# Copying a table from DRAM to DRAM instead of through SBUF, with the dst order read earlier and products of zeros in an idle stretch of TensorE

## The chip, the core and the metric

One core of one Trainium2 chip runs the kernel. The metric is the device time of one execution in microseconds (us), lower is better. The engines are TensorE (PE in the profile, PEld its weight loads), VectorE (DVE), ScalarE (ACT), GpSimd (POOL) and SyncE (SP), which only issues DMA transfers; 16 DMA engines move the data. A name with q behind it (SPq) is the engine's queue of DMA issues.

## The reference

A graph network of two layers over N = 50000 nodes with 256 features and 12500 edges; `src` and `dst` are the edges' ends, and `dst` comes sorted.

```python
h = x @ Wn.T + bn;  e = edge_attr @ We.T + be                 # layer 0, edge_attr is 12500 x 128
a = leaky_relu(sum((h[src] + e) * attn, -1), 0.01)
a = softmax of a over the edges with the same dst
z = x + relu(segment_sum(h[src] * a, dst))
x1 = layernorm(z)
mean = segment_mean(x1[dst], over the edges with the same src)  # layer 1
r = x1 + x1 @ W1.T + b1 + mean @ W2.T + b2
out = layernorm(r)
```

## The kernel before

Edges lie in T = 100 tiles of 128, four tiles make a quad, Q = 25. Nodes lie in G = 98 groups of 512, a group being 128 partitions of four rows (4 KB). All engines run in parallel, each in its own written order, held together by semaphores. The stages are:

1. *Edge features.* SyncE loads `edge_attr` in 12 blocks of eight tiles and two single ones; VectorE makes a dot product of each tile with a vector (`features`, L754), into `pay`. Before, VectorE and ScalarE make one-hots of the dst keys (`onehots`, `high_onehots`), and TensorE counts them (`sort`, first half).
2. *Sort by dst, then by src* (`sort`, `tiles`). For each quad SyncE loads the low digits of its keys (`low_digits_scratch` into `lowB`, which is part of `aggn`) and the keys (`keys_scratch` into `kB`), spread over all partitions. TensorE looks up and counts (L1228, L1179), VectorE makes ranks. GpSimd scatters each tile's (dst, src, dot) to its rank in `order_scratch` (L473), `FLIGHT` in flight, and reads the order back. The one-hots of src are made between the two.
3. *Gathers of x rows* by the dst order (`X<-in_x`, L464), `FLIGHT` in flight. They start when the dst order has been read and turned, which VectorE does in the src tiles at quad `ORDER_AT` and the two after; a row of `X` is free once the src tile in it has been counted. VectorE then makes a dot product of each tile with `v_b`, and the softmax follows.
4. *Adds* (`by_dst`). TensorE sums each quad's rows by dst and multiplies by Wn, ScalarE cuts at zero, GpSimd adds the result to rows of `z_scratch` by indirect DMA (L513), a quad after the adds of the quad before have landed.
5. *All nodes* (`dense`). Each group is loaded from `z_scratch`, normalised, turned, multiplied by W1 and I, normalised and stored. Meanwhile the src order is scattered and read (`HOOK`), and rows of z are gathered for the neighbours (`s_nb`).
6. *The rows that have edges by src* (`by_src`) once more, with the mean of the neighbours, scattered over `out`.

`z_scratch` must hold x before the first add. SyncE copies it there, a group at a time, with a load into `yout` and a store two steps later, each waiting for an earlier one (`copy`). The copy is cut up and its parts stand between SyncE's other issues: 4 steps at the start, `COPY_FIRST` ahead of the fifth block of edge features, one after the keys of two quads in three, `COPY_ONEHOTS` after the keys of the first src quad, the rest after the first two loads of the sorted dst keys. SyncE issues in this order, and what stands behind a wait waits too. GpSimd waits for the last stores ahead of its first add.

Of the kernel before, what the change touches and what calls it, by code (L numbers as in the profile page):

```python
# [20 lines left out]
BF16 = mybir.dt.bfloat16  # L21
I32 = mybir.dt.int32
DST, SRC = 0, 1
ORDER_AT = 12
FLIGHT = 4
COPY_FIRST = 12
COPY_ONEHOTS = 14
HOOK = 24


def wait(eng, sem, value):

    if isinstance(value, int) and value <= 0:
        return
    eng.wait_ge(sem, value)
# [19 lines left out]
def build(nc, x, src, dst, edge_attr, Wn, bn, We, be, attn, W1, b1, W2, b2, out):  # L55
# [12 lines left out]
    assert 2 * HC <= 512 and LO == 2 * P and T % 4 == 0  # L68
    EC = 2 * GT
    NEC = FT // EC  # L70

    z_dram = nc.dram_tensor("z_scratch", [N + 6 * P, D], F32).ap()
    keyrow_dram = [nc.dram_tensor(f"keys_scratch{k}", [T, P], F32).ap() for k in (DST, SRC)]
# [4 lines left out]
    with ExitStack() as ctx:  # L78
# [6 lines left out]
        def sems(name, n):  # L85
            return [sem(f"{name}{i}") for i in range(n)]
# [142 lines left out]
        s_sortd = sem("sorted_keys_in_dram")  # L229
        s_xones = sem("ones_columns")  # L230
        s_xg = sems("src_rows_gathered", FLIGHT)
        s_cin = sems("copy_loaded", 4)
        s_cout = sems("copy_stored", 4)
        s_zero = sem("spare_rows_cleared")

        s_xin = sems("x_loaded", 4)
# [43 lines left out]
        s_enm = sem("edge_r_scales")  # L280
        s_ey = sem("edge_y_ready")
        s_xs = sems("own_z_rows_gathered", 4)
        s_nb = sems("neighbour_z_rows_gathered", 2)
        s_zsc = sems("z_rows_added", 4)
        s_ysc = sems("y_scattered", 4)
        s_rc = sems("reciprocals", 6)
# [10 lines left out]
        def grp(dram, g, parts=P):  # L297

            if isinstance(g, int):
                return dram[g * GN:g * GN + parts * GT].rearrange("(p j) d -> p (j d)", j=GT)  # L300
            return dram[0:(G - 1) * GN].rearrange("(g p j) d -> p g (j d)", p=P, j=GT)[:, bass.ds(g, 1), :] \
                .rearrange("p a f -> p (a f)")
# [13 lines left out]
        def parts(g):  # L316
            return LP if isinstance(g, int) and g == G - 1 else P
# [4 lines left out]
        def full(ap):  # L322
            return ap[:].rearrange("p j d -> p (j d)")
# [4 lines left out]
        @block.sync  # L328
        def _(sp):
            sp.wait_ge(s_const, 1)  # L330
            for k, key in ((DST, dst), (SRC, src)):
                sp.dma_start(keyrow_i[k][0:FT, :], key[0:FT * P].rearrange("(t p) -> t p", p=P)).then_inc(s_krow[k], 16)
            for w, t in ((Wn, 0), (W1, 1), (W2, 2)):
                sp.dma_start(xin[t][:, 0:2, :], w.rearrange("(b p) k -> p b k", b=2)).then_inc(s_w, 16)
            sp.dma_start(weT, We.rearrange("(b p) k -> p b k", b=2)).then_inc(s_w, 16)

            copied = [0]

            def copy(n):

                for c in range(copied[0], min(copied[0] + n, G + 2)):
                    if c < G:
                        wait(sp, s_cout[c % 4], 16 * (c // 4))
                        sp.dma_start(full(yout[c % 4])[0:parts(c)], grp(x, c, parts(c))).then_inc(s_cin[c % 4], 16)
                    if c >= 2:
                        h = c - 2
                        sp.wait_ge(s_cin[h % 4], 16 * (h // 4 + 1))
                        sp.dma_start(grp(z_dram, h, parts(h)), full(yout[h % 4])[0:parts(h)]).then_inc(s_cout[h % 4], 16)
                copied[0] = min(copied[0] + n, G + 2)

            copy(4)
            sp.wait_ge(s_wt, 3)
            sp.wait_ge(s_vu, 1)

            for c in range(NEC):
                if c == 4:
                    copy(COPY_FIRST)
                wait(sp, s_eau, EC * (c - 3))
                v = edge_attr[0:NEC * EC * P].rearrange("(c t p) d -> p c t d", p=P, t=EC)
                sp.dma_start(full(xin[c % 4]).rearrange("p (t d) -> p t d", d=DE),  # L360
                             v[:, c:c + 1].rearrange("p a t d -> p (a t) d")).then_inc(s_ea[c % 4], 16)
            c = NEC
            for t in range(NEC * EC, FT + 1):
                rows = P if t < FT else LT
                sp.wait_ge(s_eau, EC * (c - 3))
                sp.dma_start(xin[c % 4][0:rows, 0, 0:DE], edge_attr[t * P:t * P + rows]).then_inc(s_ea[c % 4], 16)
                c += 1


            for k in (DST, SRC):  # L370
                sp.wait_ge(s_keyd[k], 32)
                for q in range(Q):
                    n = k * Q + q
                    wait(sp, s_lbT, n - 1)
                    wait(sp, s_lbA, n - 1)
                    sp.dma_start(lowB[n % 2], spread(lowrow_dram[k], q)).then_inc(s_lb[n % 2], 16)
                    wait(sp, s_kbu, n - 1)
                    sp.dma_start(full(kB[n % 2]), spread(keyrow_dram[k], q)).then_inc(s_kb[n % 2], 16)
                    if k == SRC and q == 0:
                        copy(COPY_ONEHOTS)  # L380
                    elif q % 3:
                        copy(1)

            def load3(k, q):
                if k == DST and q < 2:
                    sp.wait_ge(s_kbu, 2 * Q)
                if k == SRC and q < 2:
                    sp.wait_ge(s_sel[DST], Q)
                wait(sp, s_sel[k], q - 1)
                sp.dma_start(full(kB[q % 2]), spread(sorted_dram[k], q)).then_inc(s_kb3[k][q % 2], 16)  # L390

            sp.wait_ge(s_sortd, 16)
            for q in range(2):
                load3(DST, q)
            copy(G + 2)
            for q in range(2, Q):
                load3(DST, q)

            for u in range(4):
                sp.wait_ge(s_zsc[u], 16 * GT * len(range(u, Q, 4)))  # L400

            def dense(g, m, u):
                if in_range(g, 0, G):
                    n = parts(g)
                    if in_range(g, 4, G):
                        wait_apart(sp, s_tp, 2 * (g - 4) + 2)
                    sp.dma_start(full(xin[u])[0:n], grp(z_dram, g, n)).then_inc(s_xin[u], 16)
                if in_range(g, 5, G + 5):
                    h, hu = g - 5, (u - 5) % 4
                    n = parts(h)  # L410
                    wait_apart(sp, s_y, GT * h + GT)
                    sp.dma_start(grp(out, h, n), full(yout[hu])[0:n]).then_inc(s_yst[hu], 16)
                if isinstance(g, int) and g == G - 6:
                    sp.wait_ge(s_sortd, 32)
                    for q in range(2):
                        load3(SRC, q)
            steps(sp, G + 5, 4, 5, 12, dense)

            for q in range(2, Q):
                load3(SRC, q)  # L420
# [3 lines left out]
        def _(pool):  # L424
# [35 lines left out]
            def column(idx, t):  # L460
                return bass.IndirectOffsetOnAxis(ap=idx[:, t:t + 1], axis=0)

            def gather(dst_ap, table, where, s):
                g.indirect_dma_start(out=dst_ap, out_offset=None, in_=table, in_offset=where).then_inc(s, 16)  # L464
# [31 lines left out]
            def order_src(n):  # L496

                pool.wait_ge(s_rank, 2 * Q)
                for t in range(sent[0], min(sent[0] + n, T)):
                    scatter_order(SRC, t)  # L500
                sent[0] = min(sent[0] + n, T)

            order_src(20)
            for u in range(4):
                pool.wait_ge(s_cout[u], 16 * len(range(u, G, 4)))
            pool.wait_ge(s_zero, 48)

            for q in range(Q):
                pool.wait_ge(s_relu, 2 * q + 2)
                if q:  # L510
                    pool.wait_ge(s_zsc[(q - 1) % 4], 16 * GT * ((q - 1) // 4 + 1))
                for j in range(GT):
                    g.indirect_dma_start(out=z_dram, out_offset=column(idx_out[DST], GT * q + j), in_=xin[q % 4][:, j, :],  # L513
                                         in_offset=None, compute_op=ALU.add).then_inc(s_zsc[q % 4], 16)
                order_src(2)

            for h in range((T - sent[0]) // 2):
                pool.wait_ge(s_x1, GT * h + GT)
# [4 lines left out]
            pool.wait_ge(s_agg[DST], T)  # L523
            for t in range(T):
                pool.wait_ge(s_x1, GT * (HOOK + 8 + (G - HOOK - 14) * t // T))
                wait(pool, s_nb[t % 2], 16 * (t // 2))
                gather(X[:, t, 0:D], z_dram, column(idx_dst[SRC], t), s_nb[t % 2])

            for q in range(Q + 3):
                if q < Q:  # L530
# [209 lines left out]
        def _(dve):  # L740
# [295 lines left out]
                ins.then_inc(s_nst, 1)  # L1036

            def first_neighbours():
                for par in range(2):
                    dve.wait_ge(s_nb[par], 16 * len(range(par, T, 2)))  # L1040
                for q in range(2):
                    neighbour_stats(q, q)

# [104 lines left out]
        def _(pe):  # L1148
# [47 lines left out]
            def sort(k, after):  # L1196
# [3 lines left out]
                for t in range(T):  # L1200
# [2 lines left out]
                        pe.wait_ge(s_hotA, k * Q + t // GT + 1)  # L1203
                    count_tile(hist, t)
                nothing(hist, start=False, stop=True).then_inc(s_hist, 1)

                pe.wait_ge(s_rowtot, k + 1)
                tot = scanned[:, :, HC - 1:HC].rearrange("p b c -> p (b c)")
# [189 lines left out]
```

## Time and profile before

| | us |
|---|---|
| time before, median of 3 runs | 1667.97 (1666.65 to 1668.83) |
| the profiled execution | 1660.1 |
| its span in the profile | 1658.3 |
| TensorE busy | 1265.2 (76%) |
| VectorE busy | 1094.4 (66%) |
| ScalarE busy | 782.0 (47%) |
| GpSimd busy | 750.0 (45%) |
| granted TensorE clock, mean share of the full one | 0.901 |

The shares are means over stages with different limits, so the rows below go by stage. In a view of windows each line is a stretch in us from the span's start, with each engine's busy time and its count of instructions, the granted TensorE clock (1.00 is 2.4 GHz, 0.50 is 1.2 GHz), the mean busy share of the 16 DMA engines and what they moved. In the chain of waits a line is a start, a duration and what lasted; a DMA's duration there runs from its issue to its landing. A releaser is the event that ended an engine's idle time.

### The profile page before, as it was taken

To read this page: it belongs to the slowest core of one execution; us is meant where nothing else is said; L and a number is where in the kernel's file an instruction comes from. 1 tells how busy PE (TensorE), PEld (TensorE's weight loads), DVE (VectorE), ACT (ScalarE), POOL (GpSimd) and SP (SyncE) were. 2 spreads that over 40 slices of the span, in tenths; PEclk is the share of its full clock that TensorE was granted. 3 is DMA by queue.
4 is the path that set the end of the run, shared out by engine and by line. 5 is a ranking of instruction groups with operands and counts; after the bars stand their busy time and mean duration, and the time that the engine had idled before them with its cause. 6 is when DMAs were issued, how large, how long until landed. Compare 5 with 4: busy or idle time off the path is not lost.

```text
span 1658.3 us, 26818 instructions
## 1 busy us (share of the span) xinstructions
PE 1265.2 (76%) x7210; PEld 1068.7 (64%) x7210; DVE 1094.4 (66%) x3970; ACT 782.0 (47%) x1768; POOL 750.0 (45%) x731
## 2 busy tenths in 40 slices
PE   4277865776000799985099999999999899999994
PEld 3166754665000688764088888888888688877784
DVE  8565585666322655441088888888888888777762
ACT  6243475442000344332067777777777455444442
POOL 1035652035555678788642013333332256555553
PEclk9688798998555899999599999999999999999997
DMA  8977588767999555554557678888887323232221
GB/s 286 300 185 214 172 261 268 234 228 236 335 343 344 141 83 83 82 70 51 95 179 223 218 237 265 263 269 267 262 271 254 128 80 98 87 95 88 90 81 46
DMA packets 134006, 311.40 MB, mean 188 GB/s; under 512 B 24605, under 2 KB 57972, under 8 KB 133928
## 3 DMA queue, kind: packets, MB, share of 16 engines
q1 hardware_dynamic: 91870, 245.02, 44.7%
q0 software_dynamic: 40128, 64.45, 18.2%
q10 hardware_dynamic: 1930, 1.06, 0.2%
q8 instruction: 28, 0.46, 0.1%
q14 instruction: 50, 0.41, 0.1%
HBM read 182.23 MB, written 129.96 MB: 188 GB/s over the span
## 4 chain that ended last, share of the span: by engine, by line
PE 44%; DMA 27%; POOL 12%; issue 8%; DVE 4%; ACT 2%; SPq 2%; POOLq 0%; ACTq 0%
PE bank L1250 25%; DMA aggn<-low_digits_scratch 7%; DMA X<-in_x,idx_src 7%; PE bank L1240 6%; DMA z_scratch<-yout 5%; POOL z_scratch L513 4%; DMA xin<-z_scratch,idx_src 4%; POOL out_rows L467 4%; POOL xin L464 3%; PE bank L1247 3%; PE bank L1228 3%; DMA z_scratch<-xin,idx_out 3%; PE bank L1295 2%; PE bank L1291 2%; PE bank L1179 1%
## 5 line engine op out<-in xcount | busy, mean ns | idle before, releaser
L1250 PE MATMUL bank<-w1T,xT 128*128 128x256 f32 x1968 | 490.7, 380 | 0.0
L1250 PEld LDWEIGHTS bank<-w1T,xT 128*128 128x128 f32 x1968 | 343.3, 190 | 66.3
L473 POOL DMA_INDIRECT order_scratch<-pay,rank_i x200 | 196.8, 984 | 230.6 <-DVE rank_i L846 95.9
L568 ACT ACTIVATE yout<-bank,nmr,rstd 128x256 f32<-128x256 f32 x492 | 251.2, 576 | 8.0 <-DVE nmr L754 8.0
L919 DVE BATCH_NORM_STATS2 stats<-xin 128x6 f32<-128x512 f32 x246 | 158.7, 686 | 111.3 <-DMA xin<-z_scratch 57.6
L559 ACT COPY xT<-bank 128x512 f32<-128x512 f32 x346 | 203.0, 588 | 36.3 <-PE bank L1240 25.0
L464 POOL DMA_INDIRECT X<-z_scratch,idx_dst x100 | 94.9, 949 | 257.1 <-DVE xin L751 191.1
L919 DVE BATCH_NORM_STATS2 stats<-bank 128x6 f32<-128x512 f32 x246 | 168.5, 694 | 59.9 <-PE bank L1250 59.5
L667 ACT COPY agg<-bank 128x257 f32<-128x257 f32 (+1 forms) x200 | 74.2, 371 | 219.3 <-PE bank L1295 212.5
L513 POOL DMA_INDIRECT z_scratch<-xin,idx_out x100 | 158.2, 1582 | 40.7 <-issue 26.9
L1179 PE MATMUL bank<-X 128*128 128x196 bf16 x800 | 100.1, 261 | 99.0 <-ACT sel L654 72.8
L1228 PE MATMUL bank<-sel,agg 128*128 128x196 f32 x800 | 175.4, 369 | 0.0
L1240 PE MATMUL bank<-ident,xin 128*128 128x128 f32 x984 | 132.2, 274 | 53.1 <-DVE xin L751 53.1
L751 DVE TENSOR_SCALAR xin<-xin,stats,rstd 128x256 f32<-128x256 f32 x492 | 171.5, 410 | 1.0
L464 POOL DMA_INDIRECT X<-in_x,idx_src x100 | 97.1, 971 | 160.3 <-DVE idx_out L905 76.6
L563 ACT ACTIVATE std<-stats,eps_c 128x4 f32<-128x4 f32 x271 | 81.0, 300 | 182.0 <-DVE stats L919 173.8
L1247 PE MATMUL bank<-bias,ones 128*128 128x256 bf16 (+1 forms) x592 | 161.5, 273 | 3.0 <-ACT xT L559 2.7
L467 POOL DMA_INDIRECT out_rows<-yout,idx_out x100 | 99.9, 999 | 140.4 <-DMA xin<-z_scratch,idx_src 68.1
L1240 PEld LDWEIGHTS bank<-ident,xin 128*128 128x128 f32 x984 | 117.3, 142 | 68.3 <-issue 53.5
L1228 PEld LDWEIGHTS bank<-sel,agg 128*128 128x128 f32 x800 | 152.6, 218 | 0.3
L1179 PEld LDWEIGHTS bank<-X 128*128 128x128 bf16 x800 | 69.1, 102 | 128.2 <-ACT sel L654 86.5
L1295 PE MATMUL bank<-agg,csel 128*128 128x257 f32 (+1 forms) x396 | 123.4, 393 | 29.5 <-ACT agg L667 29.3
(187 smaller groups left out, 1911.7 us busy)
## 6 DMA issues: line engine op xcount, KB each, us to landing
yout<-in_x SPq DMA_DIRECT2D x97, 512.0 KB, 6.1
z_scratch<-yout SPq DMA_DIRECT2D x97, 512.0 KB, 7.1
xin<-z_scratch SPq DMA_DIRECT2D x97, 512.0 KB, 5.2
out_rows<-yout SPq DMA_DIRECT2D x97, 512.0 KB, 3.4
kB<-keys_scratch SPq DMA_DIRECT2D x50, 256.0 KB, 5.1
kB<-sorted_scratch SPq DMA_DIRECT2D x50, 256.0 KB, 3.4
aggn<-low_digits_scratch SPq DMA_DIRECT2D x50, 128.0 KB, 7.1
xin<-in_edge_attr SPq DMA_DIRECT2D x12, 512.0 KB, 7.1
```

Source lines behind the costliest of these rows:

```text
L464: g.indirect_dma_start(out=dst_ap, out_offset=None, in_=table, in_offset=where).then_inc(s, 16)
L473: g.indirect_dma_start(out=order_dram[k], out_offset=bass.IndirectOffsetOnAxis(ap=rank_i[k][:, t:t + 1], axis=0), in_=pay[:, t, :], in_off ...
L513: g.indirect_dma_start(out=z_dram, out_offset=column(idx_out[DST], GT * q + j), in_=xin[q % 4][:, j, :], in_offset=None, compute_op=ALU.ad ...
L559: a.copy(xT[dst_i][:].rearrange("p a b c -> p (a b c)"), src_bank[:, :]).then_inc(copied, 1)
L568: a.activation(yout[hu][0:rows, j, :], bank_of(j // 2)[0:rows, (j % 2) * D:(j % 2 + 1) * D], ACT.Identity, bias=nmr[0:rows, slot, j:j + 1] ...
L751: return v.tensor_scalar(o, i, s1, s2, o0, o1) if o1 is not None else v.tensor_scalar(o, i, s1, s2, o0)
L919: return v.bn_stats(stats[0:rows, slot, 2 * p:2 * p + 2, :].rearrange("p j s -> p (j s)"), pair.rearrange("p j c -> p c j"))
L1179: ins = mm(o[:, b * HC:(b + 1) * HC], onehot_lo[:, t, b * P:(b + 1) * P], onehot_hi[:, t, :], start=False, stop=False, skip_group_check=True)
L1228: ins = mm(bank[3 + t % 4][:, 0:HC], onehotT[n % 2][:, b, j * P:(j + 1) * P], table[i % 2][:, b, :], start=b == 0, stop=b == 1)
L1240: ins = tr(o[:, at:at + n], buf[0:n, 2 * p + jj, c * P:(c + 1) * P], ident[0:n, 0:n])
L1247: mm(to, ones16[:, 0:n], bias16[:, bias, :], start=True, stop=False)
L1250: ins = mm(to, buf[:, jj, c, 0:n], w[:, c, :], start=False, stop=i == len(terms) - 1 and c == 1)
```

## The change

The copy goes from DRAM to DRAM in NCOPY = 100 transfers, each of 125 rows of 4 KB that lie 400 nodes apart. SyncE waits for none of them; GpSimd waits for all before its first add. Eight stand ahead of the fifth block of edge features, one after each dst quad's keys, 24 after the keys of the second src quad (two at a time, as VectorE's one-hots of src progress), one after every second src quad's keys from the fourth on, and the 32 left after the first two loads of sorted dst keys. The four steps at the start are gone. `ORDER_AT` goes from 12 to 5, `FLIGHT` from 4 to 6, `HOOK` from 24 to 48; the neighbour gathers have four semaphores instead of two; GpSimd's order scatters leave the loop of the adds. After the counting of the dst keys TensorE makes 72 products of zeros into a bank that nothing reads, six after the first dot of each block.

```diff
-ORDER_AT = 12
-FLIGHT = 4
-COPY_FIRST = 12
-COPY_ONEHOTS = 14
-HOOK = 24
+ORDER_AT = 5
+FLIGHT = 6
+HOOK = 48
...
+    NCOPY = 100
...
-            copy(4)
             sp.wait_ge(s_wt, 3)
             sp.wait_ge(s_vu, 1)
+            def part_of(table):
+                return table.rearrange("(r c k) d -> c r (k d)", c=NCOPY, k=GT)
+            def copy_x(n):
+                for c in range(copied[0], min(copied[0] + n, NCOPY)):
+                    sp.dma_start(part_of(z_dram[0:N])[c], part_of(x)[c]).then_inc(s_copy, 16)
+                copied[0] = min(copied[0] + n, NCOPY)
             for c in range(NEC):
                 if c == 4:
-                    copy(COPY_FIRST)
+                    copy_x(8)
...
-                    if k == SRC and q == 0:
-                        copy(COPY_ONEHOTS)
-                    elif q % 3:
-                        copy(1)
+                    if k == DST or q >= 2 and q % 2:
+                        copy_x(1)
+                    if k == SRC and q == 1:
+                        for i in range(Q // 2):
+                            sp.wait_ge(s_onehot, Q + 2 * i + 1)
+                            copy_x(2)
...
-            copy(G + 2)
+            copy_x(NCOPY)
...
             order_src(20)
-            for u in range(4):
-                pool.wait_ge(s_cout[u], 16 * len(range(u, G, 4)))
+            pool.wait_ge(s_copy, 16 * NCOPY)
...
-                order_src(2)
...
-                wait(pool, s_nb[t % 2], 16 * (t // 2))
-                gather(X[:, t, 0:D], z_dram, column(idx_dst[SRC], t), s_nb[t % 2])
+                wait(pool, s_nb[t % 4], 16 * (t // 4))
+                gather(X[:, t, 0:D], z_dram, column(idx_dst[SRC], t), s_nb[t % 4])
...
                 nothing(hist, start=False, stop=True).then_inc(s_hist, 1)
+                if k == DST:
+                    for c in range(NEC):
+                        pe.wait_ge(s_eau, EC * c + 1)
+                        for _ in range(6):
+                            nothing(bank[0][:, 0:2 * HC], start=True, stop=True)
```

## Rows read from the trace of the kernel before

**Rows 1.** Windows view by stage; PE, PEld, DVE, ACT, POOL busy, clock, DMA share, GB/s.
```profile
22.00:87.00 65.00, 20.94 (x197) 15.91 (x194) 44.51 (x306) 33.14 (x93) 0.00 (x0) 0.77 0.96 302
87.00:225.00 138.00, 104.89 (x587) 95.33 (x588) 83.16 (x439) 56.06 (x98) 76.15 (x77) 0.82 0.67 190
225.00:282.00 57.00, 32.75 (x255) 25.59 (x254) 38.12 (x189) 39.20 (x107) 23.72 (x24) 0.89 0.95 297
282.00:409.00 127.00, 95.08 (x582) 86.10 (x580) 82.97 (x442) 53.50 (x93) 36.10 (x37) 0.92 0.72 231
409.00:564.00 155.00, 17.77 (x78) 13.24 (x79) 59.28 (x278) 6.10 (x15) 80.42 (x84) 0.55 0.91 311
564.00:822.00 258.00, 195.49 (x1032) 160.86 (x1030) 95.48 (x353) 87.33 (x188) 207.00 (x150) 0.92 0.55 72
822.00:1286.00 464.00, 456.47 (x2676) 385.28 (x2677) 408.65 (x1066) 331.46 (x758) 129.46 (x137) 0.99 0.75 247
```

**Rows 2.** SyncE's first issues; GB/s in 40 slices from 3.5 to 5.5 us.
```profile
1.13 0.35 SPq L332 DMA_DIRECT2D keyrow_i<-in_dst  x1
...
2.12 2.73 SPq L334 DMA_DIRECT2D xin<-in_L_gnn_Wn  x1
...
GB/s 5 21 25 24 24 23 32 22 22 22 22 22 21 21 32 21 21 22 23 23 24 24 33 42 42 21 21 38 41 20 31 20 20 20 20 21 20 20 20 41
```

**Rows 3.** DMA from 29 to 33 us, windows view from 28, DMA from 62 to 84.
```profile
DMA packets 447, 1.62 MB, mean 405 GB/s; under 512 B 51, under 2 KB 53, under 8 KB 446
...
28.00:44.00 16.00, 9.34 (x91) 6.95 (x88) 15.78 (x75) 16.00 (x47) 0.00 (x0) 1.00 0.96 342
...
DMA packets 9175, 6.04 MB, mean 274 GB/s; under 512 B 223, under 2 KB 8755, under 8 KB 9174
```

**Rows 4.** Timeline, chain and windows view around the edge features.
```profile
24.12 1.73 SPq L344 DMA_DIRECT2D yout<-in_x  x1
...
45.66 0.08 DVE L754 DVE_READ_ACCUMULATOR xin<-xin,u_b 128x1 f32 x1
...
54.51 0.33 PE L1175 MATMUL bank<-zero 128*128 128x392 bf16 x1
...
61.85 7.65 DMA xin<-in_edge_attr
...
80.38 3.91 DVE xin L754 x36
...
84.00:88.00 4.00, 1.69 (x5) 1.43 (x6) 2.86 (x13) 1.44 (x2) 0.00 (x0) 0.50 0.73 257
...
87.32 1.67 PE L1212 MATMUL bank<-csel,ident 128*128 128x392 f32 x2 [1.04 <-DVE csel L754]
```

**Rows 5.** Chain of waits in the dst tiles, two of its low digit loads.
```profile
155.40 7.44 DMA aggn<-low_digits_scratch
...
172.54 7.41 DMA aggn<-low_digits_scratch
```

**Rows 6.** Timeline at the start of the src tiles, ScalarE and SyncE.
```profile
282.29 0.72 ACT L606 ACTIVATE aggn<-aggn,slot_f 128x512 bf16<-128x512 bf16 x1 [3.07 <-DMA aggn<-low_digits_scratch]
...
284.06 0.32 SPq L378 DMA_DIRECT2D kB<-keys_scratch  x1
...
292.49 0.32 SPq L378 DMA_DIRECT2D kB<-keys_scratch  x1
```

**Rows 7.** The gathers of x rows, by tile X from 340 to 540 us.
```profile
L464 POOL DMA_INDIRECT X<-in_x,idx_src x100: 940/946/1196, 348.0 to 527.8; - x100
...
DMA to landing us min/median/max: 2.7/6.3/9.5
```

**Rows 8.** Timeline of GpSimd at the first add and around a quad's.
```profile
563.95 1.63 POOL L513 DMA_INDIRECT z_scratch<-xin,idx_out  x1 [4.90 <-ACT xin L680]
...
695.01 1.57 POOL L513 DMA_INDIRECT z_scratch<-xin,idx_out  x1 [0.30 <-issue]
...
699.60 1.61 POOL L513 DMA_INDIRECT z_scratch<-xin,idx_out  x1 [0.43 <-ACT xin L680]
```

More of the change, by code:

```diff
@@ L70, in build @@
     NEC = FT // EC
+    NCOPY = 100
+    assert N % (NCOPY * GT) == 0
     z_dram = nc.dram_tensor("z_scratch", [N + 6 * P, D], F32).ap()
@@ L231, in build @@
         s_xg = sems("src_rows_gathered", FLIGHT)
-        s_cin = sems("copy_loaded", 4)
-        s_cout = sems("copy_stored", 4)
+        s_copy = sem("x_copied")
         s_zero = sem("spare_rows_cleared")
@@ L282, in build @@
         s_xs = sems("own_z_rows_gathered", 4)
-        s_nb = sems("neighbour_z_rows_gathered", 2)
+        s_nb = sems("neighbour_z_rows_gathered", 4)
         s_zsc = sems("z_rows_added", 4)
@@ L335, in _ @@
             sp.dma_start(weT, We.rearrange("(b p) k -> p b k", b=2)).then_inc(s_w, 16)
[L337 to L349, printed above, removed]
-            copy(4)
             sp.wait_ge(s_wt, 3)
             sp.wait_ge(s_vu, 1)
+            copied = [0]
+            def part_of(table):
[4 more added lines that the diff above has]
+                copied[0] = min(copied[0] + n, NCOPY)
             for c in range(NEC):
                 if c == 4:
-                    copy(COPY_FIRST)
+                    copy_x(8)
                 wait(sp, s_eau, EC * (c - 3))
@@ L1038, in first_neighbours @@
             def first_neighbours():
-                for par in range(2):
-                    dve.wait_ge(s_nb[par], 16 * len(range(par, T, 2)))
+                for i in range(4):
+                    dve.wait_ge(s_nb[i], 16 * len(range(i, T, 4)))
                 for q in range(2):
```

## The prediction

> **What bounds the kernel now.** First the page: span 1658.3 us, of which TensorE 76%, no engine near full, so the stages are read apart. The windows view [rows 1] shows two kinds. From 822 to 1286 us TensorE is busy 457 of 464 us, and what comes after is touched by no edit. Ahead of it, from 22 to 564 us, no engine is full, but the DMA engines are at 0.96, 0.67, 0.95, 0.72 and 0.91. From 564 to 822 us GpSimd is busy 207 of 258 us, the most of all.
>
> The chain and the issues say what the front half waits for. From 24.1 to 61.85 us SyncE is held in the copy, whose loads and stores wait for each other; the fifth block of edge features is issued only then, lands at 69.5 us, and the dots end at 84.3 us [rows 4]. In the dst tiles one low digit load in three comes late, behind two copy pairs: its 7.4 us are on the chain once in each 17.1 us, that is three quads [rows 5]. Between the tiles of dst and of src 14 copy steps hold SyncE, and the low digits of the third src quad land at 282.3 us [rows 6]. Where no load is late two quads take 8.43 us, 4.2 each [rows 6]; over the stage it is 5.5. The x row gathers run from 348 to 534 us, four in flight at 6.3 us each [rows 7], under 311 GB/s in all [rows 1]. From 564 us a quad of adds takes 10.3 us: GpSimd 7.4 for four, then the landing of the last, under which lie two order scatters [rows 8].
>
> **The change, part by part.** *The copy.* 98 loads and 98 stores go; 100 transfers from DRAM to DRAM of 125 rows of 4 KB come. Bytes through the DMA engines fall from 102.4 to 51.2 MB, and SyncE waits for no piece. The question is how many of the 16 DMA engines a piece runs on. The rows say this depends on the count of rows: two loads of 97 rows, the first issued at 1.13 us, fill 3.5 to 5.5 us at 20 to 25 GB/s in most slices, and SyncE needs 2.73 us to issue the next load; transfers of 128 rows move 405 GB/s in 29 to 33 us, 16 times 25.3, and 274 GB/s where nearly all packets are of 512 bytes, as those of the 97 rows are [rows 2, 3]. So 97 rows ran on one engine, 128 on all. 97 is prime; the simplest reading of both is that rows are dealt out in equal shares. 125 rows then go to five engines of 25 rows. I forecast that.
>
> The Trainium skill, DMA: Bandwidth & Descriptors, on why a DMA increments its semaphore by 16, has the same as a rule: the number of engines is the largest one up to 16 that divides the slowest dimension of both sides, always the lowest-numbered. By it too this change is to be feared, and the trace's 97 rows agree.
>
> A packet of 4 KB costs an engine 162 ns at 405 GB/s and 191 ns at 342 [rows 3]; 25 of them 4.05 to 4.8 us. No row shows DRAM to DRAM. The two rates are 18% apart by nothing but how well the transfers follow each other, and pieces that wait for nothing may follow better still: I allow half of that again below, 3.7. Above, a read and a write one after the other would make 8.1 to 9.6. I take one pass and 4.4 us, the middle. Everything SyncE issues stands behind it on those five engines: key and low digit loads of a quad (384 KB) take them 1.0 us, order scatters about 0.5 (an estimate: the DMA share is 0.67 at 190 GB/s with them and 0.72 at 231 almost without, 0.08 of 138 us more than the bytes explain, over 25 quads [rows 1]).
>
> Now the sum, by stages.
> 1. *Edge features.* Eight pieces, 35 us from 24.3, behind blocks already issued: 61. The fifth block, issued at 45.7 once the first block's dots are done [rows 4], lands at 64.5 instead of 69.5: **-5 us** (-7 to -2).
> 2. *Zero products.* TensorE makes 72 of 392 columns while idle (from 54.8 us); at 0.33 us for one [rows 4] they are 24 us, spread over the dots, six after each block's first, so the last six end about with the dots. The clock is 0.50 from 84 to 88 us [rows 4]; the seed takes 1.67 us there, and half at the full clock. **-1 us** (-2 to 0; a TensorE still busy at the end would cost 1).
> 3. *Dst tiles*, one piece in each quad. Five engines: 4.4 + 1.0 + 0.5 = 5.9 us, above the 4.2 of the work, so 25 quads take 148 us against 138: **+10**. The stage ends at 229, not 225.
> 4. *Src one-hots.* SyncE issues 24 pieces ahead of the low digits of the third quad. 24 x 4.4 = 106 us, with landing and rest 109.5: these arrive at 338.5, not 282.3. ScalarE's one-hots (35 us from 226) and two quads fill only the first 45 us. **+52**.
> 5. *Src tiles* with 11 pieces. Five engines in two quads: 4.4 + 2.0, and from the eighth quad 2.5 for seven gathers; 9 us, 4.6 a quad with slips, 23 quads 107 us against 127: **-20**. They end at 446.
> 6. *To the first add.* The dst order read at quad 5 not 12 lets gathers start in the eighth quad, at 366, and six in flight let GpSimd set the pace, 0.95 us each and 0.3 between [rows 7, 8]: done by about 495, logits and softmax by 525 (30 us from the last landing to the first add, as before [rows 7, 8]). But GpSimd's adds wait for all 100 pieces, and key loads of the third and later quads are queued behind them: 32 x 4.4 = 141, gathers 12, scatters and keys 4, 1.5 to start: 604.5, where it was 563.95. 158.5 us against 155: **+3.5**. The early gathers are worth nothing here, they are 80 us ahead of the copy.
> 7. *Adds.* Without the order scatters the landing sets the pace: the last add is issued at 695.01 and lands 3.8 later by the chain, and the next quad starts at 699.60, only 0.43 after the second scatter's end [rows 8]. At most 0.3 us a quad: **-2** (-8 to 0). The 50 scatters go to the next stage, where GpSimd is busy 129 of 464 us [rows 1]; 80 of them, two a group, end at group 40, and the load of the order has eight groups of 4.7 us (464 us for 98) to HOOK 48.
> 8. *Neighbour gathers.* 100 in 36 groups rather than 60: one in 1.7 us, and GpSimd's 0.95 [rows 7] fits. DMA load there rises from about 0.8 to 0.9; TensorE covers it: 0 (to +5 if x loads come late).
>
> Sum -5 -1 +10 +52 -20 +3.5 -2 = **+37.5 us**. The profiled execution took 1660.1 us (span 1658.3), 7.9 under the median of 1667.97; I add the difference to the median: **1705.5 us**. At 4.05 us a piece the same steps give +1.5, at 4.8 us +74, so this case reaches 1669 to 1742. It breaks even near 4.03 us, 161 ns a packet: close to the best measured rate.
>
> **Rivals.** *All 16 engines.* If 125 rows are spread like 128, a piece takes 1.3 to 1.5 us. Then dots end 16 us sooner, 25 dst quads take 109 us, 24 pieces (36 us) hide under ScalarE's one-hots, src tiles end near 329 and gathers, from 254 at 1.26 us, near 385; the first add comes 30 us later at 415: -149 -2, **1517 us**. With two passes (3.0 us a piece) the copy ends at 475: **1578**. For it: no row shows a count like 125, and the one narrow case ran among the small loads of the start; against it, its flat 21 GB/s at a packet size that elsewhere gives 274. 0.22.
> *Faster on five engines.* A piece under 4.0 us: a queue of plain copies with nothing waiting between could run at the 405 GB/s slices' better half. 3.7 us gives -34, **1635**. 0.10; the 0.04 about break-even make no change.
> *Two passes on five engines.* Read and write share the engine's time: 8.1 us and more, 97 us later for each us: +397, **2065 us**. No row excludes it: in every row one side is on chip. 0.18. The Trainium skill, DMA: Bandwidth & Descriptors, latency and other measured facts, gives 214 GB/s each way for copies between HBM tensors on all engines; by that a piece on five would take 7.7 us. No run here shows it yet.
> *One engine for 125 rows*, 22 us a piece, past 3000 us: 0.01. *The move of the order matters, the copy not*: needs a copy that ends by 525, so 3.5 us a piece or all 16 engines; contained above.
>
> **How the numbers follow.** Forecast (five engines, one pass, slower) 0.42, two passes 0.18, one engine 0.01 and 0.03 for a price between one pass and two make slower 0.64; faster is 0.22 + 0.10 = 0.32; same 0.04. Within 0.2%, 3.3 us, is what a measurement here can't tell from no change. Predicted is the likeliest, 1706 us, its own range 1669 to 1742. The range of eight in ten takes in the 16-engine rival and the five-engine cases up to 5.3 us a piece: 1515 to 1790; two passes are left out.
>
> **What would show it.** In the profile after: DMA share near 5/16 = 0.31 with about 110 GB/s while only pieces run (30 to 45 us); the low digits of the third src quad landing near 338 us; GpSimd idle for over 50 us before its first add, released by the copy, near 604; gathers done near 495. A share near 1 while pieces run and a first add near 415 prove the 16-engine rival; about 65 GB/s at such a share and a first add near 960, two passes. A packet 10 ns off moves the result by 24 us, so the sign hangs on that price.

## Result and profile after

| | us |
|---|---|
| after, median of 4 runs | 1708.11 (1703.05 to 1712.09) |
| before beside it, 4 runs | 1667.64 (1666.65 to 1668.83) |
| ratio, 95% interval | 1.0241 (1.0213 to 1.0269) |
| profiled execution, span | 1703.05, 1701.3 |

Slower by 40 us, as forecast (1706, +37.5). Executions of one kernel fall into a fast and a slower state; a ratio with an interval, here and below, is of fast ones alone, a median without one is of all runs.

The windows of the kernel after, with the columns of [rows 1]:

```profile
22.00:80.00 58.00, 37.31 (x277) 23.87 (x274) 44.44 (x306) 34.54 (x97) 0.00 (x0) 0.94 0.66 195
80.00:227.00 147.00, 102.54 (x603) 91.64 (x603) 87.71 (x457) 59.27 (x107) 90.95 (x94) 0.91 0.57 155
227.00:331.00 104.00, 30.45 (x244) 23.28 (x244) 34.57 (x173) 36.36 (x100) 7.41 (x8) 0.70 0.34 125
331.00:473.00 142.00, 103.39 (x572) 95.34 (x573) 82.62 (x438) 53.12 (x93) 79.06 (x83) 0.82 0.62 176
473.00:611.00 138.00, 17.04 (x71) 11.96 (x69) 49.25 (x259) 5.57 (x13) 39.36 (x38) 0.56 0.38 145
611.00:870.00 259.00, 198.19 (x1040) 163.72 (x1040) 97.82 (x376) 88.38 (x189) 156.46 (x100) 0.92 0.54 72
870.00:1332.00 462.00, 453.58 (x2654) 382.58 (x2655) 405.80 (x1057) 329.51 (x752) 174.39 (x184) 0.99 0.74 246
```

Against [rows 1] the third stage is 104 us instead of 57, and the DMA share there is 0.34, not 0.95: the engines aren't full, yet everybody waits for a transfer. The DMA view of 30 to 45 us and of 520 to 600 us, where hardly anything but pieces runs, says how few engines work (the row of digits is the busy share of 40 slices in tenths):

```profile
DMA  3323233332323323333234332323333232332323
...
DMA packets 498, 1.97 MB, mean 132 GB/s; under 512 B 20, under 2 KB 20, under 8 KB 496
...
q1 hardware_dynamic: 496, 1.95, 32.0%
...
DMA packets 2959, 10.76 MB, mean 135 GB/s; under 512 B 264, under 2 KB 264, under 8 KB 2959
```

32.0% is 5.1 of 16 engines. Five engines at 132 GB/s are 26.4 GB/s each, or 155 ns for a packet of 4 KB. 25 packets are 3.88 us a piece, where I took 176 ns and 4.4 us. SyncE, the chain of waits and GpSimd show what stands behind the pieces:

```profile
23.90 19.27 SPq L346 DMA_DIRECT2D z_scratch<-in_x  x8
...
227.19 85.72 SPq L346 DMA_DIRECT2D z_scratch<-in_x  x24
...
472.69 120.92 SPq L346 DMA_DIRECT2D z_scratch<-in_x  x32
```
```profile
313.01 17.66 DMA aggn<-low_digits_scratch
...
390.99 10.12 DMA aggn<-low_digits_scratch
404.06 10.18 DMA aggn<-low_digits_scratch
417.03 10.82 DMA aggn<-low_digits_scratch
```
```profile
611.01 1.63 POOL L508 DMA_INDIRECT z_scratch<-xin,idx_out  x1 [87.36 <-DMA z_scratch<-in_x]
...
634.70 1.56 POOL L508 DMA_INDIRECT z_scratch<-xin,idx_out  x1 [3.04 <-DMA z_scratch<-xin,idx_out]
```

The issue of 24 pieces lasts from 227.19 to 312.91. The waits for one-hots between them can't be what holds SyncE: with the same waits the kernel with 128 rows issues its 24 pieces in 27.16 us (below). Its queue takes a new piece only as old ones move. The third src quad's low digits are issued behind it and land at 313.01 + 17.66 = 330.7, where they landed at 282.3 [rows 6]. The DMA views of 227 to 257 us and of 257 to 313 us show that these pieces began more slowly than they went on:

```profile
DMA packets 1047, 2.98 MB, mean 99 GB/s; under 512 B 316, under 2 KB 330, under 8 KB 1045
...
DMA packets 1869, 7.38 MB, mean 132 GB/s; under 512 B 70, under 2 KB 70, under 8 KB 1868
```

At 132 GB/s the first 30 us would have moved 3.96 MB, so some 7 us were lost there; why is not known. Ahead of its first add GpSimd stands 87 us for the copy. Added up from the front in the two profiled executions, in us later than before:

| place | before | after | later | forecast |
|---|---|---|---|---|
| edge feature dots end | 84.3 | 77.5 | -6.8 | -5 |
| dst tiles end | 225 | 227.2 | +2 | +4 |
| third src quad's low digits | 282.3 | 330.7 | +48.4 | +56 |
| first dot of a gathered tile, src tiles done | 408.9 | 473.9 | +65.0 | +36 |
| first add | 563.95 | 611.01 | +47.1 | +39.5 |
| first load of all nodes | 822.1 | 871.5 | +49.4 | +37.5 |
| end of the span | 1658.3 | 1701.3 | +43.0 | +37.5 |

### The profile page after: what moved, and what is told of

It is laid out like the page before. It is cut to its first block, busy times and chain, and to the rows that moved or that the text cites. A ratio compares the mean times of both kernels' runs of the same rounds, so it can differ in the third digit from the quotient of the medians.

```text
span 1701.3 us, 26861 instructions
## 1 busy us (share of the span) xinstructions
PE 1287.3 (76%) x7282; PEld 1083.0 (64%) x7282; DVE 1088.1 (64%) x3970; ACT 783.1 (46%) x1768; POOL 747.7 (44%) x731
## 4 chain that ended last, share of the span: by engine, by line
PE 36%; DMA 23%; POOL 12%; SPq 12%; DVE 8%; issue 7%; ACT 2%; POOLq 0%; ACTq 0%; DVEq 0%
PE bank L1249 23%; DMA aggn<-low_digits_scratch 12%; SPq L346 11%; PE bank L1239 6%; POOL z_scratch L508 6%; DMA z_scratch<-xin,idx_out 5%; POOL out_rows L463 4%; DMA xin<-z_scratch,idx_src 3%; DVE X L745 3%; POOL xin L460 3%; PE bank L1246 3%; PE bank L1294 1%; PE bank L1227 1%; DMA xin<-in_edge_attr 1%; PE bank L1290 1%
## 5 line engine op out<-in xcount | busy, mean ns | idle before, releaser
L913 DVE BATCH_NORM_STATS2 stats<-xin 128x6 f32<-128x512 f32 x246 | 158.5, 686 | 94.0 <-DMA xin<-z_scratch 56.6
L1290 PE MATMUL bank<-X,sel 128*128 (+2 forms) x400 | 123.7, 393 | 80.1 <-DVE csel L745 80.1
L1227 PE MATMUL bank<-sel,agg 128*128 128x196 f32 x800 | 179.4, 375 | 0.0
L1227 PEld LDWEIGHTS bank<-sel,agg 128*128 128x128 f32 x800 | 156.1, 222 | 0.3
```

Source lines behind the costliest of these rows:

```text
L913: return v.bn_stats(stats[0:rows, slot, 2 * p:2 * p + 2, :].rearrange("p j s -> p (j s)"), pair.rearrange("p j c -> p c j"))
L1227: ins = mm(bank[3 + t % 4][:, 0:HC], onehotT[n % 2][:, b, j * P:(j + 1) * P], table[i % 2][:, b, :], start=b == 0, stop=b == 1)
```

## Experiments

Three groups of four kernels, each group on one chip with before beside it. The first ran where before took 1656.68 us (1649.49 to 1664.59, 7 runs). In the second and third, on two other chips, before took 1729.12 (1677.02 to 1744.02) and 1720.37 us (1687.30 to 1753.12). In all eight profiles taken there the chain of waits from 60 to 600 us has 8 to 23% in "another core or an unknown queue", in the six of the first two chips nothing. So those kernels are compared with each other alone, without interval.

### First group: rows of a piece, place of the order, zeros

**128 rows.** The piece's rows, and nothing else: 97 pieces of 128 rows and one of 84.

```diff
-    NCOPY = 100
+    NCOPY = G
...
-                return table.rearrange("(r c k) d -> c r (k d)", c=NCOPY, k=GT)
+                if c == G - 1:
+                    return grp(table, c, LP)
+                return table[0:(G - 1) * GN].rearrange("(r c k) d -> c r (k d)", c=G - 1, k=GT)[c]
```

> The changed kernel, but with pieces of 128 rows (97 of them, and one of 84) at the same places. Theory (rows are dealt out in equal shares, so 125 rows ran on five engines and 128 run on 16; a packet costs 155 ns as in the changed kernel): a piece takes 1.3 to 1.5 us, the DMA share is near 1 and the rate near 400 GB/s from 25 to 33 us, the low digits of the third src quad land near 230 us, the first add comes near 415 us when the gathers and the softmax are done, and the time is 1520 to 1560 us. Rival (a copy from DRAM to DRAM is slow for another reason, such as reads and writes of the same memory, at 132 GB/s whatever the rows): the rate stays at 132 GB/s and the time near 1708 us. Rival two passes at 16 engines (3 us a piece): the first add near 475 us and 1578 us.

**1520.85 us** (1517.93 to 1523.14), ratio 0.9175 (0.9138 to 0.9213). Its DMA view from 30 to 38 us, its first add, and its windows for three of the stages:

```profile
DMA packets 786, 2.88 MB, mean 359 GB/s; under 512 B 88, under 2 KB 88, under 8 KB 784
...
q1 hardware_dynamic: 784, 2.85, 101.8%
```
```profile
428.31 1.63 POOL L509 DMA_INDIRECT z_scratch<-xin,idx_out  x1 [9.82 <-ACT xin L675]
```
```profile
180.00:234.00 54.00, 33.46 (x273) 26.18 (x271) 39.36 (x197) 39.60 (x108) 22.93 (x24) 0.95 0.96 257
234.00:341.00 107.00, 88.87 (x573) 80.18 (x573) 81.59 (x439) 53.43 (x93) 60.15 (x62) 0.94 0.71 211
341.00:422.00 81.00, 11.23 (x46) 7.73 (x46) 53.44 (x267) 3.73 (x9) 58.79 (x59) 0.56 0.75 269
```

All 16 engines are busy, the 24 pieces are issued in 27.16 us instead of 85.72, and the copy is gone from GpSimd's wait: the first add waits 9.8 us for the last step of its own chain. The number of engines that a piece runs on, not the copy from DRAM to DRAM as such, is what the change lost by.

**100 rows.** The changed kernel with `NCOPY = 125`, so pieces of 100 rows: more and smaller pieces, of a count that shares out over ten engines.

> The changed kernel with 125 pieces of 100 rows: the same numbers of pieces at the same places, 57 instead of 32 at the end. Theory (the largest number of engines up to 16 that divides the rows, so 10): 10 packets of 155 ns, 1.55 us a piece of 410 KB, 264 GB/s and a DMA share of 0.63 while only pieces run; first add near 437 us, about 1545 us. Rival (rows are cut into 16 shares rounded up, 15 engines of 7 rows, and 125 rows ran on five for another reason): 1.1 us a piece, 377 GB/s, share 0.94. Rival (five engines whenever the rows are no multiple of 16): 3.1 us a piece, 132 GB/s, share 0.32, and 1700 us or more.

**1541.21 us** (1539.51 to 1546.06), ratio 0.9303 (0.9262 to 0.9344). Its DMA view from 30 to 40 us, and its first add:

```profile
DMA packets 703, 2.63 MB, mean 263 GB/s; under 512 B 63, under 2 KB 63, under 8 KB 702
...
q1 hardware_dynamic: 702, 2.62, 64.3%
```
```profile
442.99 1.63 POOL L508 DMA_INDIRECT z_scratch<-xin,idx_out  x1 [30.18 <-DMA z_scratch<-in_x]
```

64.3% is 10.3 engines at 26 GB/s. So 125, 100 and 128 rows run on 5, 10 and 16 engines: equal shares, as the prediction read from 97 rows. The Trainium skill (DMA: Bandwidth & Descriptors, on why a DMA increments its semaphore by 16) states this as a rule, and these three runs agree with it. At ten engines GpSimd still waits for the copy, 30 us, and the kernel takes 20 us longer than on 16.

**Order at quad 12.** The changed kernel with `ORDER_AT = 12`.

> The changed kernel with ORDER_AT 12 as before. Theory (the copy on five engines ends last, everything about the gathers is ahead of it): the gathers of x rows start near 415 us instead of 364 and end near 545, the first add still comes at 611 us within 4, and the time is the same within 0.2%, 1705 to 1711 us. Rival (the early gathers crowd the five engines in the src tiles and slow the low digits there): the src tiles end 10 to 20 us sooner, and if the pieces after them aren't slower by the same, the time falls by as much.

**1709.41 us** (1707.21 to 1713.12), ratio 1.0308 (1.0263 to 1.0353). The windows and the first add:

```profile
326.00:461.00 135.00, 95.69 (x563) 87.17 (x564) 80.75 (x432) 53.51 (x93) 44.35 (x47) 0.86 0.52 150
461.00:611.00 150.00, 18.82 (x81) 13.61 (x78) 53.70 (x264) 5.56 (x13) 72.12 (x74) 0.56 0.46 164
```
```profile
611.66 1.63 POOL L508 DMA_INDIRECT z_scratch<-xin,idx_out  x1 [56.29 <-DMA z_scratch<-in_x]
```

Gathers begin at 398.0 instead of 363.7, and the first add comes at the time that the changed kernel had on the first chip. The late order moves time: the src tiles are 135 us instead of 142 with fewer gathers in them, and the stretch to the first add is 12 us longer. That the early order is worth nothing on five engines is not shown by this, since no run of the changed kernel stands beside it on that chip: by the ratios to before (1.0308 and 1.0241, the intervals just overlap) quad 12 is 11 us slower. The kernel without zeros, next, has its order at quad 5 and ran on the same chip. It issues the low digits of the third src quad at the same time (309.04 against 308.87), and has its first add at 602.85, 9 us before the one with quad 12 (one profiled execution of each, and its own was the fastest of its four); the medians are 6 us apart, with runs that just overlap. So the early order may be worth some 6 to 11 us even here. A likely reason is that with quad 12 more of the gathers share the engines with the last 32 pieces: 52 of them are issued between the first dot and the first add, and 18 in the changed kernel.

**No products of zeros.** The changed kernel without them:

```diff
-                if k == DST:
-                    for c in range(NEC):
-                        pe.wait_ge(s_eau, EC * c + 1)
-                        for _ in range(6):
-                            nothing(bank[0][:, 0:2 * HC], start=True, stop=True)
```

> The changed kernel without the products of zeros. Theory (they only warm the seed: 1.10 us against 1.67 us): the time is the same within 0.1%, at most 1 us longer. Rival (they keep TensorE's clock up into the dst tiles, where low digit loads are late): the dst tiles take several us longer without them, 1711 us or more.

**1703.49 us** (1698.26 to 1708.27), ratio 1.0282 (1.0235 to 1.0329). The one product behind the dots, in this kernel and in the changed one:

```profile
79.70 1.68 PE L1206 MATMUL bank<-csel,ident 128*128 128x392 f32 x2 [1.03 <-DVE csel L748]
```
```profile
80.09 1.10 PE L1211 MATMUL bank<-csel,ident 128*128 128x392 f32 x2 [1.03 <-DVE csel L748]
```

The zeros save 0.58 us there. The rival, a clock held up through the dst tiles, can be judged by the kernel with quad 12, which has the zeros and ran on the same chip. With and then without zeros the 24 pieces behind the dst tiles begin at the same time:

```profile
225.40 83.36 SPq L346 DMA_DIRECT2D z_scratch<-in_x  x24
...
224.83 84.10 SPq L346 DMA_DIRECT2D z_scratch<-in_x  x24
```

So the dst tiles are no longer without them, and that rival fell. For the total the interval overlaps the changed kernel's 1.0241, and a difference of a few us can't be told: no run of the changed kernel on that chip stands beside it.

### Second group: what limits it once the copy is quick

**The changed kernel again.**

> The changed kernel once more, beside the kernels with 128-row pieces and on the chip that runs them. If the zero products do nothing but heat TensorE's idle time, it is within 0.3% of the kernel without them, whose ratio was 1.028; if they hold the clock up behind the edge features, it is 4 us and more below that one. From the first measurement the ratio should be 1.024, some 40 us above before. The fixed part of each stage (dst tiles 147 us, src tiles 142 us, first add near 611) should come again within 2 us, since five DMA engines set them.

**1819.15 us** (1796.35 to 1824.08) where before took 1729.12: 1.052, and stages came later by tens of us, so the expectation of the same stages failed; the one on the zeros can't be judged across chips. A piece was no dearer (DMA from 30 to 40 us: 131 GB/s at 31.8%), but the first add came at 656.69.

**128 rows, order at quad 12** (`ORDER_AT = 12`).

> Pieces of 128 rows on all 16 engines, but the dst order read at quad 12 of the src tiles as in the kernel before. Theory: on five engines the early order was worth nothing because the copy ended 80 us behind the gathers; with the copy done by 240 us the gathers end last before the adds, so seven quads of 4.3 us later costs 25 to 30 us, less some 4 us because the src tiles are crowded by fewer gathers: 1543 to 1550 us against 1521 (ratio near 0.934), first add near 455. Rival: the order is worth nothing here either, since the gathers are bounded by the rows of X that the src tiles free: 1521 to 1525 us, first add near 430.

**1705.42 us** (1698.43 to 1727.52), first add at 542.79, where 1543 to 1550 and 455 were expected. The kernel with quad 5 and HOOK 48 did not run on this chip; the next one has quad 5, but HOOK 24.

**128 rows, order scatters back in the adds, HOOK 24:**

```diff
-HOOK = 48
+HOOK = 24
...
                                          in_offset=None, compute_op=ALU.add).then_inc(s_zsc[q % 4], 16)
+                order_src(2)
```

> Pieces of 128 rows, but the two order scatters of src stand between the quads of the adds again and the order of src is turned at group 24. Theory: the scatters lie under the landing of the adds, whose gap of 2.9 to 3.2 us in the version without them hardly shortens, so 25 quads give back 3 to 8 us: 1524 to 1529 us; the dense stage stays at 462 us, since TensorE sets its pace. Rival: the scatters cost nothing at all (1521), or the later order also eased DMA in the dense stage and its return makes this 10 us and more (1531 or over).

**1672.64 us** (1657.21 to 1682.70), first add at 524.21. The total has no partner here, so the pace of the adds has to decide. GpSimd's first add of two quads in this kernel, and in the one without the scatters:

```profile
741.93 1.61 POOL L509 DMA_INDIRECT z_scratch<-xin,idx_out  x1 [0.47 <-ACT xin L676]
...
752.11 1.61 POOL L509 DMA_INDIRECT z_scratch<-xin,idx_out  x1 [0.41 <-issue]
```
```profile
645.77 1.56 POOL L509 DMA_INDIRECT z_scratch<-xin,idx_out  x1 [3.06 <-ACT xin L675]
...
655.98 1.56 POOL L509 DMA_INDIRECT z_scratch<-xin,idx_out  x1 [3.05 <-DMA z_scratch<-xin,idx_out]
```

These are 10.18 and 10.21 us a quad, and over all 25 quads the mean is 10.35 with the scatters and 10.34 without: the scatters fill a gap of 3 us that the landing leaves anyway. In the adds the rival "nothing at all" holds, mine of 3 to 8 us fell.

**128 rows, order at quad 1, 16 pieces among the one-hots:**

```diff
-ORDER_AT = 5
+ORDER_AT = 1
...
-                        for i in range(Q // 2):
+                        for i in range(8):
                             sp.wait_ge(s_onehot, Q + 2 * i + 1)
                             copy_x(2)
```

> Pieces of 128 rows, the dst order read at quad 1 of the src tiles instead of 5, and 16 pieces instead of 24 among the one-hots of src (the other eight come after the sorted dst keys). Theory: the gathers set the first add, so four quads of 4.3 us earlier give 17 us, and eight pieces fewer ahead of the third quad's low digits up to 8 us more: 1496 to 1504 us, first add near 408. Rival: a row of X is free only when the src tile in it has been counted, so the gathers are held to the tiles' pace of 1.07 us each and more tiles of crowding slow the tiles: no more than 5 us won, 1515 to 1521, or slower.

**1662.41 us** (1651.77 to 1662.60), first add at 491.42: 43 us below the one with quad 12 and 10 below the one with quad 5 and HOOK 24. It differs from both by more than the order.

### Third group: four of them repeated

> The changed kernel, repeated beside its relatives, since on the last chip before itself spread from 1677 to 1744 us and loads there landed late. On a quiet chip: ratio 1.024 as first measured, first add near 611. If the ratio is 1.05 again, the changed kernel suffers more than the one before from whatever made that chip slow.

> Pieces of 128 rows, repeated as the base for the two below. Expected 0.9175 of before, 1521 us on a quiet chip, first add near 428.

> Pieces of 128 rows and the order read at quad 12. Theory: the gathers end last before the adds, so it is 25 to 30 us above the version with quad 5 (1546 to 1551), first add near 455. Rival: no difference, within 4 us of it.

> Pieces of 128 rows, the order read at quad 1, 16 pieces instead of 24 among the one-hots of src. Theory: 17 us from the gathers and up to 8 from the one-hots, 1496 to 1504 on a quiet chip, first add near 408. Rival: gathers held to the pace of the tiles, no more than 5 us won.

| kernel | us | gathers from, to | first add |
|---|---|---|---|
| changed | 1827.26 (1780.85 to 1843.89) | | 658.4 |
| 128 rows, order at 5 | 1672.89 (1670.69 to 1713.32) | 295.7 to 438.6 | 518.4 |
| 128 rows, order at 12 | 1703.77 (1663.71 to 1709.68) | 330.6 to 471.8 | 542.0 |
| 128 rows, order at 1, 16 pieces | 1645.28 (1627.41 to 1659.11) | 277.5 to 422.1 | 495.7 |

The medians step by 31 and 28 us, first adds by 24 and 23. The step from quad 5 to quad 1 with 16 pieces is clear of the runs' spread in this group (1659.11 at most against 1670.69 at least), and near the 17 to 25 us of the theory; what the order and what the eight pieces give of it was not taken apart. The step from quad 12 to quad 5 is not clear: one run with quad 12 took 1663.71, less than any with quad 5. For a gain from quad 5 speak the second group, where the one with quad 12 is 33 us above the one with quad 5 and HOOK 24 (1698.43 at least against 1682.70 at most), and first adds that move the same way, by 19 and 24 us. So on 16 engines the early order is probably worth something; the 25 to 30 us of the theory are not shown, and the mechanism is not cleanly the one expected. The windows of the tiles and of the stretch behind them, with quad 5 and then with quad 12:

```profile
255.00:436.00 181.00, 110.24 (x631) 97.08 (x632) 88.37 (x467) 59.32 (x105) 93.20 (x97) 0.80 0.58 175
436.00:489.00 53.00, 0.38 (x3) 0.00 (x0) 36.95 (x203) 0.00 (x0) 23.19 (x23) 0.55 1.00 313
```
```profile
257.00:468.00 211.00, 108.68 (x636) 96.58 (x637) 87.31 (x464) 60.97 (x110) 93.31 (x97) 0.75 0.52 154
```

The last gather is issued at about the time the tiles end, and only then does VectorE begin its 100 dots. What grew is the tiles' own stage, 211 us against 181 (on the chip of the first group 107), while gathers run in it. But gathers aren't all of it: the dst tiles, which have none, are slow there too, for the first piece behind them is issued at 222.54 us with quad 5 and 228.42 with quad 12, and at 185.86 with quad 5 on the chip of the first group. Why tiles are so slow on these chips stays open. One sign is in the kernel with quad 1 of the second group: between 149 and 152.4 us its DMA engines are idle,

```profile
DMA packets 64, 0.00 MB, mean 1 GB/s; under 512 B 64, under 2 KB 64, under 8 KB 64
```

and the chain has there, where the low digits should land,

```profile
146.48 5.85 another core or an unknown queue
```

so the release comes 3 to 4 us behind the last data that the trace shows. The quick version with quad 1 wasn't run on the chip of the first group; what it gives there (expected: 1496 to 1504) is not shown.

## Why the prediction was right

**Five engines, one pass: right.** The step on which the sign hung. Equal shares hold for 125, 100 and 128 rows, and a DRAM to DRAM copy has no second pass: 359 GB/s on 16 engines counts each byte once, near the 342 to 405 of [rows 3]. The rival of two passes is dead. The Trainium skill (DMA: Bandwidth & Descriptors, latency and other measured facts) gives 214 GB/s each way at best for copies between HBM tensors with 16 KiB in a partition; the copy here, with 4 KB in a row, is above that, and the measurement decides. The rival of all 16 engines was false for 125 rows, but its steps can be judged by the kernel with 128. In units of the first measurement that is 0.9175 x 1667.64 = 1530 us against its 1517, and its last step, the first add near 415, came at 428.

**The size was right by luck: errors of opposite sign cancelled.**
- *Price of a piece*, forecast 4.4 us, measured 3.88. The prediction called 4.03 the break-even and gave -34 us at 3.7; at 3.88, between its +1.5 at 4.05 and -34, the same steps give about -16. The kernel lost 40 at that price, so the break-even was wrong, and the steps had some 56 us too little at the true price. The condition of the rival that is faster on five engines, a piece under 4.0 us, came true; its time of 1635 us did not.
- *Step 5, src tiles*, forecast -20 us, measured +16.6 (330.7 to 473.9, against 282.3 to 408.9): the mis-sized term, 37 us. I counted what five engines must move for two quads, 4.4 + 2.0 us and 2.5 for gathers. The rows say latency: nine low digit loads stand on the chain of after in the src tiles from 344 us on, at 7.8 to 10.8 us each, since a load is issued only when its buffer comes free and then stands behind a piece and a key load. With quad 12, before any gather starts, two quads take 10.5 us where five engines have only 3.88 + 2.0 us to move (with the prediction's estimate for the key loads). With gathers it is 12.5 on average. It was already so in before, at 7.9 to 9.7 us a load once gathers run. With pieces of 128 rows, which move in 1.5 us at 359 GB/s, such loads take 5.6 to 6.8 us: the piece in front is what the chain pays for, more than the engines' fullness.
- *Steps 3 and 4* came out near the forecast, but not for its reason alone: dst tiles end at 227.2 (229), the third quad's low digits land 48 us later (56). With the 49 pieces of these two stages at 3.88 us, the same steps would give 135 us for the dst tiles and 97 for the one-hots; measured are 147 and 103.5. In the dst tiles too the low digit loads stand on the chain, at 8 to 11 us, where they took 6.5 to 8.4; in the one-hots it is the slow start seen above.
- *Step 6* was the other side. The stretch from tiles to first add took 138 us, not 158.5, because the 32 pieces were cheaper and only 18 gathers lay in it. The 12 us forecast for gathers are 34 of them, at the 2.5 us for seven of step 5. By the table of lateness step 5 lost 37 us on the forecast, step 6 won 21 and step 4 won 6. The cheap piece hid most of what the loads' landing cost.

**The small terms.** Edge features -6.8 (-5), zeros about -0.6 (-1). *Step 7*: taking the order scatters out gave nothing. From the third quad on a quad takes 10.34 us on average, where it took 10.32, and the second one starts at 624.48, 13.5 us after the first, since its sums are late. The chain shows why:

```profile
593.66 17.72 DMA kB<-sorted_scratch
```

This key load, the first behind the last piece, lands at 611.4, and the chain then runs through TensorE, not GpSimd, to 666 us. In the six profiles where GpSimd waits for the copy the second quad comes 13.5 to 14.9 us after the first, in the seven with 128 rows 10.2 to 10.3. The net is +2, not -2. *Step 8*: the dense stage is 462 us instead of 464 and the rest is 6 us shorter in all; what of it comes from the spread gathers was not tested.

**What the early order was for.** The prediction said that it is worth nothing on five engines. No run shows that cleanly: quad 12 on another chip left the first add where it was, but beside its neighbour on the same chip it is 9 us late. On 16 engines the medians speak for some 30 us, in two groups with overlap or a second difference between the kernels.

## What to carry to other kernels

Before a transfer is cut into pieces, look at the count of its rows: three more rows in a piece (128 for 125) made this copy 2.7 times as fast and the kernel 10% faster. A slow transfer on an in-order queue costs each load behind it its landing time, so price it by the chain of waits and not by the bytes that the engines could move. And a total that comes out right can hide wrong terms: compare stage by stage.

## What was not expected of the hardware

- A 4 KB packet from DRAM to DRAM takes 155 ns (26.4 GB/s an engine), less than the 162 to 191 ns of loads and stores in [rows 3].
- SyncE issues eight pieces in 19.27 us on five engines, 7.01 on ten and 6.17 on 16: the queue holds the issuing engine back long before a semaphore does.
- On two of the chips before itself was 3 to 4% slower by its median and spread over 66 and 67 us; by medians of all runs the changed kernel lost 5 to 6% there, and the 16-engine one won only 3% on the one where it ran.
